# First block turned and split tile by tile, its score seeds written by TensorE, gate and up weights copied in halves, tanh of the first two blocks written to SBUF

## What is computed

```python
xn  = (x - mean) / sqrt(var + 1e-5)
# attention branch
h   = tanh(xn @ W1.T + b1)                     # 256 -> 256
s   = h @ w2.T + b2                            # one score for each token
e   = exp(s - max(s))                          # max over the whole sequence
ctx = cumsum(e * xn) / cumsum(e)               # along the sequence
a   = tanh(concat(ctx, xn) @ Wc.T + bc)
# feed-forward branch, weights are int32 times 1/127
g, u = xn @ wg.T, xn @ wu.T                    # 256 -> 768
f   = (silu(g) * u) @ wd.T                     # 768 -> 256
out = x + a + f
```

## Time and profile before

| | us |
|---|---|
| median of 3 runs | 393.87 |
| lowest and highest | 393.25, 393.88 |
| profiled execution, its own time | 393.06 |
| its span (first to last instruction) | 391.1 |
| PE busy in the span | 385.9 |

### The profile page before, as it was taken

How to read it: one execution, slowest core, us unless ns; L and a number is a source line. 1 busy time by engine, 2 the same in 40 slices (tenths; PEclk the granted TensorE clock), 3 DMA queues, 4 the chain that set the end, 5 groups by cost and what they waited for, 6 DMA issues and landing times.

```text
span 391.1 us, 7885 instructions
## 1 busy us (share of the span) xinstructions
PE 385.9 (99%) x2740; PEld 268.7 (69%) x2740; DVE 297.5 (76%) x632; ACT 235.6 (60%) x434; POOL 210.1 (54%) x289
## 2 busy tenths in 40 slices
PE   8999999999999999999999999999999999999996
PEld 4556676757566686866877676767677676676765
DVE  6799998999996997876769966777676765754351
ACT  4766576689985659786556575364553644536250
POOL 1487586874629989794335405866456554502000
PEclk9999999999999999999999999999999999999999
DMA  8944525576834232475210005043231220100001
GB/s 275 348 158 69 137 53 134 106 189 89 201 72 96 54 83 81 116 165 97 76 34 29 27 28 164 28 128 87 58 72 55 90 85 26 54 28 28 28 28 61
DMA packets 54945, 36.56 MB, mean 93 GB/s; under 512 B 31858, under 2 KB 50292, under 8 KB 54900
## 3 DMA queue, kind: packets, MB, share of 16 engines
q1 hardware_dynamic: 54608, 35.73, 35.5%
q10 hardware_dynamic: 292, 0.26, 0.2%
HBM read 20.19 MB, written 8.45 MB: 73 GB/s over the span
## 4 chain that ended last, share of the span: by engine, by line
PE 97%; DVE 2%; issue 0%; DVEq 0%
PE bank L707 44%; PE bank L743 41%; PE bank L763 9%; PE bank L1381 1%; DVE ex L1121 0%; DVE stats L951 0%; PE bank L700 0%; PE bank L1377 0%; DVE veps L980 0%; DVE xt L1091 0%; DVE bank L1116 0%; DVE sg L1413 0%; PE bank L813 0%; DVE mv L955 0%; PE bank L819 0%
## 5 line engine op out<-in xcount | busy, mean ns | idle before, releaser
L743 PE MATMUL bank<-xt,narrow 128*128 128x512 f16 x768 | 177.3, 379 | 0.0
L743 PEld LDWEIGHTS bank<-xt,narrow 128*128 128x128 f16 x768 | 75.2, 98 | 75.4 <-DVE wide L1121 0.2
L707 PE MATMUL bank<-narrow,wide 128*128 128x256 f16 x792 | 96.4, 273 | 0.0
L707 PE MATMUL bank<-narrow,xt 128*128 128x256 f16 x768 | 92.8, 273 | 0.3 <-DVE xt L1091 0.3
L707 PEld LDWEIGHTS bank<-narrow,xt 128*128 128x128 f16 x768 | 75.0, 98 | 19.0 <-DVE xt L1091 0.6
L1258 POOL TENSOR_TENSOR wide<-ex,wide 128x512 f16<-128x512 f32 x32 | 39.4, 1248 | 87.6 <-ACT wide L909 87.6
L888 ACT ACTIVATE sg<-bank 128x512 f32<-128x512 f32 x96 | 57.2, 596 | 46.3 <-PE bank L743 45.6
L1116 DVE SCALAR_TENSOR_TENSOR bank<-bank,sg 128x512 f32<-128x512 f32 x96 | 66.1, 694 | 24.4 <-PE bank L743 21.3
L707 PEld LDWEIGHTS bank<-narrow,wide 128*128 128x128 f16 x792 | 77.5, 98 | 9.4
L895 ACT ACTIVATE wide<-bank 128x512 f16<-128x512 f32 x90 | 53.3, 596 | 47.7 <-DVE bank L1116 39.3
L1121 DVE TENSOR_TENSOR wide<-bank,wide 128x512 f16<-128x512 f32 x90 | 60.5, 678 | 9.9 <-ACT wide L895 8.6
(11 more groups left out here) (103 smaller groups left out, 262.3 us busy)
## 6 DMA issues: line engine op xcount, KB each, us to landing
rows<-scratch SPq DMA_DIRECT2D x16, 512.0 KB, 5.1
out_y<-xres SPq DMA_DIRECT2D x31, 256.0 KB, 2.1
xres<-in_x SPq DMA_DIRECT2D x15, 512.0 KB, 5.1
xt<-xt SPq DMA_TRANSPOSE x56, 2.5
wide<-in_wg SPq DMA_DIRECT2D x1, 768.0 KB, 5.9
wide<-in_wu SPq DMA_DIRECT2D x1, 768.0 KB, 8.4
wide<-in_wd SPq DMA_DIRECT2D x1, 768.0 KB, 10.1
wide<-in_wc SPq DMA_DIRECT2D x1, 512.0 KB, 11.1
```

Of the source, the lines that this page charges most:

```text
L707: return pe.matmul(dst, lhs, rhs, start=False, stop=stop, skip_group_check=True)
L743: mm = pe.matmul(b[:, :], pg.up(which, k, j), pg.xn(sx, k, tok), start=n == 0, stop=n == len(todo) - 1)
```

## The change

**Block 0 tile by tile.** The steps `Lb`, `Xh`, `Xl`, `Ss` of block 0 go. `L0`, `X0`, `Y0` take their place, each four times for one tile: two transposes, a high half of 2x128 columns by ACT, a low half by DVE. `first_scores` runs the high products of all four tiles, then the products with the low half of W1, then the low products of pair 0, and those of pair 1 only after one `Gg`.

**Bias seeds of block 0.** PE writes them itself: four products of one row (`up_row`, filled with the scale) with the row of b1. The 12 warm-ups become 6, the two between the turns and the scores go. ACT no longer sends the row of w2, and `Ea` is gone: b1 and w2 come to `every` as broadcast transfers of 128 KB each on SP's queue, b1 behind wu, w2 behind block 2 of x.

**Inverse root of block 0.** ACT takes the root of variance plus eps in one instruction from `mv`, so that DVE's step `veps` goes.

**Weights in halves.** `Wgh` and `Wuh` are two instructions each, of three sixths of the hidden features, and PE waits for the half that it needs.

**Tanh of blocks 0 and 1** is written to `rows` in SBUF (`AWAY = 2`). `Th` frees the bank in place of `Sv`, and `Sv` of these blocks, which reads `rows`, has a due time 25 us after the scores in place of 0.8.

```diff
+AWAY = 2
-    "Wgh": (PO, 1.5, 1.6), "Wuh": (PO, 1.5, 1.6), ...
+    "Wgh": (PO, 0.77, 0.87), "Wuh": (PO, 0.77, 0.87), "L0": (TE, 0.22, 0.35), "X0": (SE, 0.31, 0.43), "Y0": (VE, 0.36, 0.49), ...
-            due["Th", i, pr], due["Sv", i, pr] = end["S", i, pr] + 0.1, end["S", i, pr] + 0.8
+            due["Th", i, pr], due["Sv", i, pr] = end["S", i, pr] + 0.1, end["S", i, pr] + (25.0 if i < AWAY else 0.8)
...
+                if kind == "S" and i < AWAY:
+                    return a_s, self.nth("Th", i, n)
...
+        def turn_tile(pe, t):
+            pe.wait_ge(v_xn, t + 1)
+            for k in range(KD):
+                mm = pe.transpose(bank_of(fits, "L0", 0, t)[:, k * P:(k + 1) * P], xnat[:, t // 2, t % 2, k * P:(k + 1) * P], ident[:, :])
+            mm.then_inc(p_x0, 1)
+
+        def first_scores(pe, pr):
+            def onto(t, sx, sw, stop=False):
+                for k in range(KD):
+                    mm = pe.matmul(bank_of(fits, "S", 0, t // 2)[:, t % 2 * D:(t % 2 + 1) * D], fits.xn(sx, k, slice(t * P, (t + 1) * P)),
+                                   fits.w1(sw, k), start=False, stop=stop and k == KD - 1, skip_group_check=True)
+                return mm
+            if not pr:
+                pe.wait_ge(a_w, 1)
+                for t in range(4):
+                    pe.wait_ge(a_x0, t + 1)
+                    onto(t, 0, 0)
+                pe.wait_ge(v_w, 1)
+                for t in range(4):
+                    onto(t, 0, 1)
+            for t in (2 * pr, 2 * pr + 1):
+                pe.wait_ge(v_x0, t + 1)
+                mm = onto(t, 1, 0, True)
+            mm.then_inc(p_s, 1)
...
             elif kind == "Ss":
-                act.wait_ge(a_b, 1)
                 act.wait_ge(p_warm, 1)
+                act.wait_ge(s_b1, 16)
...
-                act.activation(b[:, :], b[:, :], ACT.Tanh, scale=1.0 / pg.sum_up).then_inc(a_s, 1)
+                act.activation(rows[:, i, n, :] if i < AWAY else b[:, :], b[:, :], ACT.Tanh, scale=1.0 / pg.sum_up).then_inc(a_s, 1)
...
             dve.wait_ge(v_mv, 2)
-            step(dve.tensor_scalar(veps[:, t], mv[:, t, 1], EPS, None, ALU.add))
-            dve.tensor_scalar(minus_half[:, t], veps[:, t], -0.5, None, ALU.mult)
+            dve.tensor_scalar(minus_half[:, t], mv[:, t, 1], EPS, -0.5, ALU.add, ALU.mult)
...
             elif kind == "Sv":
                 if (i, n) == (0, 0):
-                    dve.wait_ge(a_b, 1)
+                    dve.wait_ge(s_w2, 16)
                 dve.wait_ge(a_s, pg.nth("Th", i, n))
...
             sp.dma_start(half(wu32.bitcast(I32)), rows_of(wu)).then_inc(s_wu, 16)
+            sp.dma_start(b1_every, biases[0:D].partition_broadcast(P)).then_inc(s_b1, 16)
             sp.dma_start(wd32.bitcast(I32).rearrange("p (k n) -> p k n", k=KH), rows_of(wd)).then_inc(s_wd, 16)
             load_x(sp, 2)
+            sp.dma_start(w2b, w2b2_in[0:D].partition_broadcast(P)).then_inc(s_w2, 16)
             sp.dma_start(wc_32, rows_of(wc)).then_inc(s_wc, 16)
...
-            act.dma_start(w2_row, w2b2_in[0:D].rearrange("(o d) -> o d", o=1)).then_inc(s_w2, 16)
...
-            for n in range(WARM):
-                mm = warm_up(n % BANKS)
+            def seed_first(n):
+                for t in range(2):
+                    pe.matmul(bank[n][:, t * D:(t + 1) * D], up_row[:, :], b_row, start=t == 0, stop=False, skip_group_check=True)
```

195 lines of the change are left out of this document (112 added, 83 removed).

## The result

The changed kernel took 395.74 us (median of six runs, 395.16 to 396.61), the kernel before 393.88 in the same session (six runs, 393.25 to 394.20). The ratio is 1.0055 with a 95% interval of 1.0043 to 1.0066: slower by 1.9 us, where 1.1 was forecast. The profiled execution of the changed kernel took 396.61 us, 0.9 above its median; the one of before took 393.06. So the traces lie 3.55 us apart, and half of that is this execution's own.

The account below looks back on a forecast made before the run. PE bounds the kernel, busy 385.9 of 391.1 us. Gains of 1.1 and 0.33 against waits of 2.5 lose 1.1, so the median 393.87 becomes 395.0; range 392.3 to 396.2.

Parts of the forecast that it names:

- signs of being wrong: Listed beforehand: w2 before 15.5, H(0,0) at 15, no PE idle at 19, scores after 8.5, rows at twice the pace.
- part 2: DVE's Sv(0,0) waits for w2, landing at 16.6; H(0,0) starts at 18.1, not 16.35, and Xl(1,0) 1.1 us later.
- the faster rival: At Sv(0,0) on DVE: w2 lands before 15.5, the start's gain is kept, -1.2 to -1.4 us, 392.6; chance 0.19.
- Part 1: The start on PE: block 0's scores are through 1.1 us earlier, with bounds of 0 and 1.3.
- the pace of the seeds: PE's one-row bias seeds: about 2.3 us, twice that at half the clock, ending between 6.4 and 8.6; lower end taken.
- the clock rival: PE still slow when block 0's scores start, through fewer warm-ups and one-row products: +2.2 us on top, 397; chance 0.09.
- w2's landing: On SP's queue behind block 2: 16.6, with 0.39 us for each 128 KB broadcast; bounds 15.8 and 17.3.
- Who waits: PE runs ten groups of 0.86 us, stands ready for Gg(0,5) at 19.3 and waits 1.3 for Hl(0,0).
- gains of 1.1 and 0.33: On PE: 1.1 us won at the start, and 0.33 from the old wait for Xl(1,0).
- waits of 1.3 + 0.5 + 0.7: PE's new waits: for Hl(0,0) ahead of Gg(0,5), for Xh(1,0), and for Xl(1,0) ahead of block 1's low products.
- the rule on the shared ports: VectorE with two SBUF inputs contends with GpSimd reading SBUF: Sv beside POOL a few tenths dearer, left out of the sum.
- The rule on the order within a ring: Each DMA engine takes a ring's descriptors in order, so w2 lands behind block 2; weighed against w2 landing early.

Follow-up runs that it names:

- e2: Changed kernel with twelve warm-up products ahead of the seeds in place of six; 1.6 us over the kernel before.
- e9: Changed kernel with its seed products over 128 rows in place of one (block 0's bias wrong), w2 still late; 395.28 us, ratio 1.0047.
- e13: Changed kernel with seeds padded to 128 rows and no broadcast of b1, w2 in its late place; 395.07 us, ratio 1.0045.
- e7: Changed kernel with block 0's seeds left to ACT, b1 broadcast early on ACT's queue, w2 behind wu, 14 warm-ups; 394.09 us.
- e8: e7 with w2 sent behind block 2 again, nothing else; 395.43 us.
- e10: Changed kernel with seeds over 128 rows (b1 in row 0 of a zeroed tile) and w2 sent behind wu; 392.86 us, ratio 0.9987.
- e3: Changed kernel with both w2 sent directly behind wu and twelve warm-ups in place of six; ratio 1.0004 to the kernel before.
- e1: Changed kernel with the broadcast of w2 sent directly behind wu, nothing else; 395.54 us.
- e4: Changed kernel with the planner placing both Sv of block 0 behind H(1,0) on DVE; ratio 1.0074 to the kernel before.
- e11: e10 with two more warm-up products, eight in all; 393.19 us, ratio 0.9991 to the kernel before.

## Why the prediction came out as it did

**The number came out in the range, the path that was told did not.** 395.74 lies near 395.0, and the kernel is slower, as forecast. But three of the prediction's own signs of being wrong are in the trace: the score row begins at 10.57, and anything after 8.5 was to mean that the start is wrong; rows after 6 us stand at twice the time of the full pace; and PE's row at 19 us has no idle time. In the changed kernel PE isn't early and waiting, it is late by its clock, and w2's wait ends at the same moment. The wait of part 2 is real all the same. With the clock up it is the only cost left, and e2, e9 and e13 then lie 1.6, 1.9 and 1.7 us over the kernel before; e7 and e8 price w2's place at 1.3 us, and between e9 and e10 it is 2.4, which is also the distance between the forecast and the faster rival (395.0 and 392.6). So the number holds because the clock's cost, which the prediction priced at 2.2 us on top, is hidden by that wait and adds next to nothing. That it hides whole is luck.

**Part 1 failed at its second step, the pace of the seeds.** It took the lower end of its bounds, "the clock had risen before 6.11, and the seeds should see that too". They did not: 3.75 us, the upper end. The mistake was to carry a clock that twelve full warm-ups had brought up over to a start with six and twice as many one-row products behind them. Twelve warm-ups ahead of the one-row seeds (e2, e3) or full rows in the seeds behind six (e9, e10) brought it up in time. The bounds 6.4 to 8.6 for the end of the seeds held (8.04). The forecast gave the clock rival 0.09 and thought of it as an addition of 2.2 us on top. In fact it stood beside w2's wait: PE late by its clock reaches the same `H` that w2 holds, and the two overlap almost wholly. e1 and e2 show that each alone costs nearly all of it. With it fell the gain of 1.1 us on PE, which is there only with the clock up, and then is 0.7.

**The rest of the start, with the clock up (e9, e10).** Turns end near 8.5, not 8.1; the scores start at 8.37 to 8.44; the products behind them come 0.7 to 0.75 earlier, not 1.1. ACT's four high halves took 1.28 to 1.66 us, 0.32 to 0.41 each, within the bounds of 0.27 and 0.54. DVE is free for `Sv` at 13.4 (e9), not at 12.7, which costs nothing while it waits for w2. The halves of wg and wu, the removed `Ea` and tanh in SBUF cost nothing that any run shows.

**w2's landing was mis-sized** by the broadcast of b1, 1.0 to 1.4 us for 0.39, and moves by another 1.7 us with the landing of wg (8.0 in e9, 9.7 in e4). With the 8.6 from wg to w2 that e9 has, and wg as before at 8.6, the estimate would have been 17.2 and the forecast 395.6.

**Who waits was named one step too late.** The prediction let PE run ten groups and wait ahead of `Gg(0,5)` for `Hl(0,0)`. It ran nine and waited ahead of `Gu(0,4)`, whose bank `Gg(0,3)` had held: `Sg(0,3)` frees it, needs the silu buffer that `H(0,0)` gives back, and stands on ACT behind two high halves of `H`. In e9 these are `H` at 18.07, two halves from 18.79, `Sg(0,3)` at 19.88, PE at 20.53.

**The balance.** The prediction set gains of 1.1 and 0.33 against waits of 1.3 + 0.5 + 0.7 = 2.5. In e9 the gains were 0.7 and 0.33, the waits 1.54, 0.09 (ahead of the row at 24.09) and 0.53, in sum 2.2. Both sides had been taken 0.3 to 0.4 too large, and so the difference was right: that is luck in the terms, not precision. `veps` of block 2 took 0.17, as predicted once POOL's copy of wd doesn't lie beside it (21.55 to 23.02, `veps` at 26.20).

**The three rules that were weighed.** By the rule on the shared ports (the Trainium skill, SBUF — State Buffer) the prediction expected `Sv` from SBUF to be dearer by a few tenths beside POOL. From the first `Sv` to the `H` behind it went 1.49 us in the changed kernel and 1.41 in e9, no more than the 1.49 from a bank. It was POOL's step beside the first `Sv` that took longer, 0.49 us, where its neighbours took 0.20 to 0.25; in e10 and e9 the step beside it took 0.44 and 0.33, in e2, where it began just ahead of `Sv`, 0.20. That agrees with a lock, but the other side paid:

```profile
17.73 0.20 POOL L1068 TENSOR_TENSOR rstd<-rstd,newton 128x4 f32<-128x4 f32 x1
18.01 0.49 POOL L1070 TENSOR_TENSOR shift<-mv,rstd 128x4 f32<-128x4 f32 x1
18.58 0.25 POOL L1071 TENSOR_SCALAR shift<-shift 128x4 f32<-128x4 f32 x1
```

The rule on the order within a ring (the Trainium skill, DMA: Bandwidth & Descriptors, Queues, rings and completion order) agrees with the traces: w2 landed behind block 2 in every one that had it there. What the Trainium skill, TensorE: Matmul & The Clock Gate, Part 4, says on transposes was weighed for the clock rival; in the traces of e9, e10, e11 and e13 the same eight turns ran and the clock stayed up through them, so the turns alone didn't decide; what ran ahead of them did.

**The faster rival** was priced at 392.6 for a w2 that lands before 15.5. e10 is that case with the clock up, and gave 392.86: the gain is 0.85 in the profiled executions and 0.5 in the medians, for the 1.2 to 1.4 priced.

## What to carry to other kernels

Read the pace of the same instruction in several rows before costing a start, and treat warm-up work as part of the cost: what replaces it must keep the clock up, not only fill the time. When a change has two side effects that end at the same instruction, undoing either shows nothing; undo both before giving up on either. Price a small transfer on a full queue by what one like it took there, not by its bytes. And a trace is one execution: set its time beside the others of the same kernel before taking it for all of them.
